# Up products directly behind the gate products of the same rows, in TensorE's order of the last stage

## The reference

```python
n3 = layernorm(x)                                      # 256 x 256
Q, K, V = n3 @ Wq.T + bq, ctx @ Wk.T + bk, ctx @ Wv.T + bv
context = einsum(softmax(K over rows), V)              # per head
x = x + tanh(g_xattn[1]) * ((Q . context) @ Wo.T + bo)
h = layernorm(x)
scores = sigmoid(h @ Wr); the two largest of scores + bias give weights cw
g, u = h @ Wg[e], h @ Wu[e]                            # 4 experts, 256 -> 128 each
hid = silu(g) * u
routed = sum over e of cw[e] * (hid @ Wd[e]) + cw[4]*h + cw[6]*h + cw[7]*relu(h)
x = x + tanh(g_ffn[1]) * (routed + causal convolution of h with 4 taps)
```

## Time and profile before

| what | us |
|---|---|
| median of 3 executions | 2349.99 (2345.68 to 2351.77) |
| the profiled execution's own time | 2349.05 |
| its span, first to last instruction | 2346.0 |
| TensorE (PE) busy | 2232.9 (95%) |
| VectorE (DVE) busy | 1801.9 (77%) |
| ScalarE (ACT) busy | 1286.3 (55%) |
| GpSimd (POOL) busy | 654.9 (28%) |
| mean granted TensorE clock | 0.985 |

### The profile page before, as it was taken

One profiled execution on the slowest core, in us unless ns is written; L12 is line 12 of the kernel. 1 busy time (PEld: TensorE's weight loads), 2 busy tenths in 40 slices (PEclk: granted clock), 3 DMA queues, 4 the chain that ended last, 5 costly groups with the idle time before them and its releaser, 6 DMA issues. The chain is left out here.

```text
span 2346.0 us, 52900 instructions
## 1 busy us (share of the span) xinstructions
PE 2232.9 (95%) x15232; PEld 1872.2 (80%) x15232; DVE 1801.9 (77%) x6078; ACT 1286.3 (55%) x3250; POOL 654.9 (28%) x1162
## 2 busy tenths in 40 slices
PE   5999999999999999999679999999699999999998
PEld 4777777777777777777479999999678888888887
DVE  4888888888888888888655555555388898988997
ACT  5776676676676676676333333333244554444454
POOL 1133223223223223222200000000255555555542
PEclk9999999999999999999789999999899999999999
DMA  5310010010010010000052222221212121211110
GB/s 185 111 55 29 27 37 27 28 36 28 27 36 27 28 36 27 28 30 19 14 174 82 82 82 81 76 67 42 75 52 61 60 60 60 60 60 56 59 45 19
DMA packets 111574, 128.47 MB, mean 55 GB/s; under 512 B 14915, under 2 KB 98362, under 8 KB 111281
## 3 DMA queue, kind: packets, MB, share of 16 engines
q1 hardware_dynamic: 98576, 103.81, 13.9%
q0 software_dynamic: 12288, 21.21, 3.1%
q10 hardware_dynamic: 544, 1.57, 0.2%
HBM read 84.39 MB, written 54.53 MB: 59 GB/s over the span
## 5 line engine op out<-in xcount | busy, mean ns | idle before, releaser
L485 ACT ACTIVATE a_prob<-a_prob,a_nmax 128x376 f32<-128x376 f32 x512 | 307.2, 605 | 25.9 <-DVE a_nmax L641 25.6
L1326 ACT ACTIVATE e_hidden<-e_first,e_b 128x256 f32<-128x256 f32 x320 | 133.9, 471 | 287.5 <-PE e_first L80 284.7
L1000 PEld LDWEIGHTS a_turned<-a_ident,a_prob 128*128 128x128 f32 (+1 forms) x1536 | 176.5, 140 | 140.6 <-issue 98.7
L1000 PE MATMUL a_turned<-a_ident,a_prob 128*128 128x128 f32 (+1 forms) x1536 | 266.6, 283 | 14.5 <-DVE a_probT L660 11.0
L641 DVE CUSTOM_DVE_ANT_0 a_prob<-a_score,a_mask_row 128x376 f32<-128x376 f32 x512 | 262.3, 540 | 20.7 <-DVE a_lg L722 9.7
L493 ACT ACTIVATE a_probT<-a_turned 128x384 f32<-128x384 f32 x256 | 125.8, 491 | 224.2 <-PE a_turned L1000 218.7
L80 PE MATMUL e_first<-e_rowsT,e_w 128*128 128x256 f32 x1920 | 239.2, 285 | 1.5 <-issue 1.5
L653 DVE TENSOR_SCALAR a_prob<-a_prob,a_rden 128x376 f32<-128x376 f32 x512 | 238.7, 492 | 2.2
L80 PE MATMUL e_second<-e_w,e_hidden 128*128 128x256 f32 x1920 | 239.7, 285 | 0.0
L80 PEld LDWEIGHTS e_first<-e_rowsT,e_w 128*128 128x128 f32 x1920 | 235.5, 194 | 1.7 <-issue 1.7
L80 PEld LDWEIGHTS e_second<-e_w,e_hidden 128*128 128x128 f32 x1920 | 232.7, 192 | 0.0
(11 more groups left out here) (204 smaller groups left out, 4846.6 us busy)
## 6 DMA issues: line engine op xcount, KB each, us to landing
slots<-a_zeros SPq DMA_DIRECT2D x8, 1280.0 KB, 9.0
e_rows<-slots SPq DMA_DIRECT2D x40, 256.0 KB, 4.0
answers<-e_y SPq DMA_DIRECT2D x40, 256.0 KB, 2.3
a_xn<-x SPq DMA_DIRECT2D x32, 256.0 KB, 3.0
a_xr<-x SPq DMA_DIRECT2D x32, 256.0 KB, 2.8
x<-a_x SPq DMA_DIRECT2D x32, 256.0 KB, 2.8
w_in<-W SPq DMA_DIRECT2D x16, 512.0 KB, 4.0
e_w_in<-W SPq DMA_DIRECT2D x16, 512.0 KB, 4.2
```

Source lines behind the costliest of these rows:

```text
L485: nc.scalar.activation(prob[:, u % 4, a], prob[:, u % 4, a], ACT.Exp, bias=nmax[:, u % 4, a:a + 1], scale=-1.0, accum_out=den[:, u % 4, a: ...
L1000: last = nc.tensor.transpose(turned[0:hi - lo, j * P:(j + 1) * P], prob[:, u % 4, a, lo:hi], ident[:])
L1326: nc.scalar.activation(hidden[:, 2 * j + i], first[:, j, i * CH:(i + 1) * CH], ACT.Relu, bias=b1[:, 2 * j + i, bass.ds(e, 1)]).then_inc(re ...
```

## The change

TensorE's `step` in `finish` issues the two up products at other places; nothing else differs. The up products of half 0 move ahead of `logits`, directly behind the gate products of half 0. The up products of half 1 move from behind `keys` of the next step (there batch s - 4) to the end of the step, directly behind the gate products of half 1 (batch s - 3).

```diff
@@ -2228,8 +2228,6 @@
                 if live(s - 2):
                     turn3(s - 2)
                     keys(s - 2)
-                if live(s - 4):
-                    gate_up(s - 4, 1, 1)
                 if live(s - 3):
                     turn4(s - 3, q)
                 if live(s - 2):
@@ -2241,11 +2239,10 @@
                     context(s - 2)
                 if live(s - 3):
                     gate_up(s - 3, 0, 0)
+                    gate_up(s - 3, 0, 1)
                     logits(s - 3)
                 if live(s - 2):
                     attended(s - 2)
-                if live(s - 3):
-                    gate_up(s - 3, 0, 1)
                 if live(s - 4):
                     turn_hid(s - 4, 1)
                 if live(s - 2):
@@ -2254,6 +2251,7 @@
                     add_rest(s - 4, 0)
                 if live(s - 3):
                     gate_up(s - 3, 1, 0)
+                    gate_up(s - 3, 1, 1)
```

## The result

| | before | after |
|---|---|---|
| median, us (8 runs each, side by side) | 2349.68 (2345.68 to 2354.93) | 2359.06 (2355.11 to 2364.34) |
| ratio after / before, 95% interval | | 1.0040 (1.0027 to 1.0054) |
| the profiled execution's time, its span | 2349.05, 2346.0 | 2355.11, 2353.1 |
| PE busy | 2232.9 (95%) | 2233.3 (95%) |
| DVE busy | 1801.9 (77%) | 1795.9 (76%) |

The change costs 0.40%, by the interval 6.3 to 12.7 us. The forecast was 18: slower was right and the time lies in the range, but the size is only about half of what was worked out.

The account below looks back on a forecast made before the run. TensorE's own work was taken as the bound: 19.50 + 0.37 + 0.62 = 20.49 us a step against 20.055. Steady steps +9.6, seven others +6.1, start +2.3, end +1.5: +19.5, written as 2368 us, range 2355 to 2377.

Parts of the forecast that it names:

- The bound: Steady step of the last stage: 20.055 us, 19.50 TensorE's own work, 0.555 waiting for VectorE's v and x3.
- The query wait: Half 1's up products gone from behind keys: queries held by ScalarE's xT until 5.64 us, +0.37 a step.
- The output wait: Half 0's up products gone from behind attended: output held by aT, 1.82 us after attended, +0.62 a step.
- Lower plane of x4T: Input of half 0's gates: ready at 9.6 us of the step, gates at 9.78, so covered by 0.1 us.
- later logits: Logits, router and x3 come 1.47 us later behind the gates; cost 0, at most 0.28 us a step.
- x4h: VectorE's input to turn4: ready at 4.85 to 4.9 us of the step, with x2k ended before it starts.
- 1: Rival: both new waits stay away and today's go; step 19.50 us, total about 2338; chance 0.06.
- 2: Rival: only the wait ahead of output comes, xT being in time; step 20.12 us, about 2358; chance 0.13.
- 4: Rival: new gaps cost TensorE its clock; price from nothing to a doubling of 19.50 us; chance 0.01.
- 5: Rival: starts only trade places, both waits at half size, step 20.05 us, nothing changes; chance 0.04.
- 3: Rival: VectorE's chain late too (x4h tied to x2k, or x4T's lower plane); 2374 to 2380 us; chance 0.14.
- two ends: Start and end of the last stage: +2.3 us for steps 3 and 4, +1.5 at the end; suspect if only the total misses.

Follow-up runs that it names:

- xt_first: Changed kernel with ScalarE making xT ahead of hidT of half 0; 2376.65 us, ratio 1.0017 to the kernel before.
- half0_only: Kernel before with only the up products of half 0 moved, ahead of the logits; 2354.06 us, ratio 1.0023 to the kernel before.
- rest_first: Changed kernel with add_rest of half 0 moved ahead of output; 2371.71 us, ratio 0.9991 to the kernel before.
- logits_between: Changed kernel with the logits back between gate and up products of half 0; one execution, 2357.95 us.
- half1_only: Kernel before with only the up products of half 1 moved, to the step's end; 2349.38 us, ratio 0.9993 to the kernel before.
- three_in_a_row: Changed kernel with half 0's up products between gate and up products of half 1 at the step's end; one execution, 2368.26 us.
- both_fixes: Changed kernel with xT ahead of hidT and add_rest of half 0 ahead of output; 2368.10 us, ratio 0.9985 to the kernel before.
- half1_xt_first: Kernel before with only half 1's up products moved and xT ahead of hidT; 2366.13 us, ratio 0.9978 to the kernel before.

## Why the prediction was right or wrong

- **The bound.** Right: 19.50 us of TensorE's own work and 0.555 of waiting. Both waits of before, for v and x3, are gone from the view of waits.
- **The query wait, +0.37.** Right to 0.02 us: queries at 5.62 for 5.64, 1.99 us long. xt_first took it away alone, and with it the 0.10.
- **The output wait, +0.62.** Right to 0.03: 1.79 behind attended for 1.82. half0_only shows it alone, rest_first covers it.
- **Lower plane of x4T covered by 0.1, later logits free.** Right: 0.11 to 0.17 us of cover, and logits_between gained nothing.
- **x4h.** Right that POOL's x2k doesn't hold it (0.73 us). Its time is 0.1 to 0.15 late: ready at 5.00 for 4.85 to 4.9, because VectorE starts line 1936 at 3.60 and not at 3.45. "keys end at 4.94 [...] and turn4 stands there now" is therefore wrong by 0.12; turn4 starts at 5.06. The sum doesn't feel it, since the queries wait for xT until 5.62 anyway; xt_first did.
- **The size of the step, wrong.** The sum "19.50 + 0.37 + 0.62 = 20.49 us" took every up product as "six matmuls and takes 2303.23 - 2301.76 = 1.47 us", a duration read behind f32 products. Two groups a step now stand directly behind gates and take 1.38: -0.18. The two waits were read 0.05 too long. 20.49 - 0.18 - 0.05 = 20.26, measured 20.245. For half 0 the error sits in the output wait, seen from the rows: its up group took 1.57 us before and not 1.47, attended ahead of it 0.76 and now 0.94. So what is left between attended and output is 0.94 + 0.44 = 1.38 us and not "1.30", and the wait 1.79 - 1.38 = 0.41 and not "0.52". TensorE's own work shrank by the 0.09 of half 1 alone. Over 29 steps the 0.245 are 7.1 of the 7.4 us that the forecast of +19.5 has too many against +12.1. The other parts of the sum held: the head +2.2 for +2.3, the tail +1.3 for +1.5.
- **The total.** The ratio gives +9.4 us and the two profiles +12.1 in the last stage; the ratio's interval (6.3 to 12.7) holds both. The "two ends" that the prediction named as a second suspect aren't at fault.
- **Rivals.** 1, 2, 4 and 5 are out: both waits came, the clock is 1.00. 3 did not happen in the changed kernel, but it makes every second step long in five variants (half1_only, three_in_a_row, rest_first, both_fixes, half1_xt_first). The rule of the Trainium skill (GPSIMD Engine Reference, section 8, Key points) of contention on the shared interfaces: the trace of half1_only agrees where the two overlap (x4h 1.19 us beside x2k, 0.73 without); which of the two conditions x4h meets is not shown. The forecast that x2k ends before x4h starts held in every second step of the changed kernel; in the others they overlap by 0.17 us, at no cost.

The change loses because the two up products were the cover of two round trips of 1.8 us (attended to output) and 2.8 us (the last products into total, 2102.24, to the queries, 2105.06) over ScalarE. What it frees, VectorE's slack ahead of v and x3, was worth 0.555 us a step, and what it uncovers about 0.75, the shorter group of half 1 already taken off.

## What to carry to other kernels

Before moving a long group of matmuls, list which round trips over another engine start ahead of it and end behind it, and compare the trip with what stays in between: both new waits came out within 0.03 us that way. Waits of one pipeline are bounds beside each other and don't add: half 0 alone cost 0.107 us a step, half 1 alone gained 0.163, together they cost 0.19. Take a group's duration from a place where the same kind of group stands ahead of it, and take it together with its neighbours, since time between starts moves from one to the other.

## What the runs showed of the hardware that was not expected

- Six matmuls of 512 columns on fp32r operands take 1.47 us from start to start behind an f32 group of 8, 120 or 128 columns, and 1.38 behind another fp32r group of 512 columns, also one of other rows (2.75 for two). Behind an f32 group of 256 columns they take 1.57 (behind attended in before, behind output in rest_first), and that group is shorter by up to 0.18.
- A product group whose start was held by a semaphore is 0.10 us longer for the same eight matmuls (1.99 against 1.89), and with the wait removed it is 1.89 again (xt_first).
- A VectorE instruction that begins while POOL issues an indirect DMA, with a POOL tensor-tensor right behind it, was held until that one ended or up to 0.5 us longer: 2.34 us for 0.61, 2.63 for 0.73, and 1.49 for 0.16 on 2 columns. Beside x2k alone x4h took up to 1.25 us instead of 0.73, and ended 0.48 us behind it. POOL's spans in the profile are rough, and what holds VectorE is not shown.
